# New queue order at image borders, and the gates' inner layer computed by rows of 512 pixels with stationary weights, turned through DRAM scratch

## Chip, cores and metric

One NeuronCore of a Trainium2 chip runs the whole kernel. The metric is the device time of one execution in microseconds (us). Engines: PE is TensorE, PEld its weight loads, DVE is VectorE, ACT is ScalarE, POOL is GpSimd, SP is SyncE, which issues every DMA of this kernel. TensorE's clock is granted by the chip at one of two levels, 1.2 or 2.4 GHz.

## The reference, cut to what matters

Eight images of 128 channels and 128x128 pixels pass two layers. The change touches layer 0 only; of it, the gates of the spectrum matter here:

```
x = x + _fssa(_gn(x), ...)      # layer 0, image by image
x = x + _L1_conv_ref(_gn(x))    # layer 1, a scan over the pixels
def _fssa(x, ...):
    xf = jnp.fft.fft2(x)
    ...                          # attention between channels of xf, softmax -> out_f
    g = _conv(xf.real, w1, b1)   # inner layer: 128 channels to 8, 1x1
    g = batch_norm(g); g = relu(g)
    g = sigmoid(_conv(g, w2, b2))    # 8 channels to 128
    out_f_l = abs(ifft2(g * xf))
    ...                          # q, k, v by 3x3 and 5x5 convolutions, attention, projections
```

As w1 works on channels and the transform on pixels, the kernel applies w1 to the normalised pixels first and transforms the 8 resulting channels.

## The kernel before, in words

Layer 0 handles one image after another. Each engine has one in-order program written out by hand: a function `image(b, more)`, run in a hardware loop for images 0 to 6 and once more in straight line for image 7. Engines meet at semaphores. Between images 6 and 7 there is thus no jump; after each of images 0 to 5 every engine jumps back to the top of its program.

The stages of one image, in order:

1. **Forward transform.** Per step t of 32 (four channels each), PE does `stage1(t)`: four matmuls of columns of x (`xh`, 16 channels a buffer, two buffers, loaded by SP's `columns(e, i)`) with the table `fwd` into bank t%2. ACT copies it into `AB`. `stage2(t)` makes imaginary and real part of the spectrum. DVE's `xi_copy` (L758, L759) and `xr_copy` (L764, L765) scale them into `XI`, `XR`, which lie in the SBUF tile `region`. Meanwhile the padded image `xpad` (2 MB in each of four row blocks, L1086) is normalised in place by ACT after steps 4, 12, 20 and 28.
2. **Gram.** PE multiplies the spectrum with itself, 256 matmuls of 128 columns in fp32 and some edges.
3. **Inner layer.** 128 matmuls, one a pixel column c: stationary is `xpad[:, 2:130, 2+c]` (128x128), moving is `w1t` with 8 columns. The output has rows of the image on partitions. ACT copies it to `T8`, eight matmuls with `fwd` follow, DVE copies to `A8`, `B8` (L798, L799), ten more matmuls give the 8 channels' spectrum; ACT makes the ReLU.
4. **Softmax and gates.** DVE reads the Gram (L803 to L825), with small matmuls and ACT operations between. Then five groups of gate matmuls (`gate_w`), ACT Sigmoid, DVE multiplication of XR and XI by the gates (L835).
5. **Inverse transform**, 64 matmul groups; then a loop over 32 groups of rows that mixes heads in the frequency domain and leaves `OF` in `region` (s_of).
6. **Stores and loads.** SP stores OF to DRAM as `heads` in three parts (L1111), the parts `region[kept[1]:kept[2]]` (1920 KB), `[0:kept[1]]` (1152 KB), `[kept[2]:HW]` (5120 KB). Then it loads kernels over them: WB, for the 5x5 convolutions, over the first part (L1114), WA over the second (L1116), WV and WC over the third (L1119). PE waits for WB (s_wl). ACT waits for the third store (`s_ofst[2]`) before it writes `VP[1]`, which lies there.
7. **q and k convolutions** (16 steps j), small attention, kernel merging, and the **output convolutions** (16 steps, `finish` on DVE, L1043 makes x1, L1045 its statistics). SP's `store` (L1139) writes x1.

The end of an image, in SP's order:

```
if more:
    sp.wait_ge(s_pf.sem, s_pf.at(b, NJ))
    sp.wait_ge(s_lf.sem, s_lf.at(b, NJ))
    start(b + 1)                      # four column DMAs, four xpad DMAs
sp.wait_ge(v.sem, v.at(b, LINKS))     # all of DVE's links of this image
store(NK - 1, 1)
sp.dma_start(gn2[...], col(4, 2)).then_inc(s_gst, 16)
```

DVE's next image begins with a wait for `s_gst`, since `small` and x1's buffers (in `region`) must have been read out. In the traces most matmuls carry the helper's line L1160.

Of the kernel before, what the change touches and what calls it, by code (L numbers as in the profile page):

```python
# [29 lines left out]
ACT = mybir.ActivationFunctionType  # L30
# [100 lines left out]
def layer0(nc, B, x, table, shift_d, w, wts, y_d, of_d, x1, gn2):  # L131
# [3 lines left out]
    with ctx:  # L135
# [64 lines left out]
        T8 = wk(5120, 1024).rearrange("p (w j) -> p w j", j=JG)  # L200
# [346 lines left out]
        s_t8 = count("s_hidden", 2)  # L547
        s_t8c = count("s_hidden_copied", 2)
# [111 lines left out]
        def _(dve):  # L660
# [52 lines left out]
            def image(b, more):  # L713
                n, pn, an = [0], [0], [0]

                def link(op):
                    n[0] += 1
                    op.then_inc(v.sem, 1)
                    dve.wait_ge(v.sem, v.at(b, n[0]))

                def mark(name):
                    VL[name] = n[0]
# [30 lines left out]
                dve.wait_ge(s_gst, b * 16 + 16)  # L753
# [41 lines left out]
                for hf in range(2):  # L795
                    dve.wait_ge(s_h1.sem, s_h1.at(b, hf + 1))
                    src = bk[2 + hf][:, :].rearrange("p (j u) -> p u j", j=4)
                    link(V.tensor_copy(A8[:, :, 4 * hf:4 * hf + 4], src[:, 0:HALF, :]))  # L798
                    V.tensor_copy(B8[:, 1:64, 4 * hf:4 * hf + 4], src[:, HALF:, :]).then_inc(s_h1c.sem, 1)  # L799
# [26 lines left out]
                mark("f_mix")  # L826
                for g in range(NUG):
# [243 lines left out]
        def _(sp):  # L1071
# [10 lines left out]
            def start(e):  # L1082
                for i in range(2):
                    columns(e, i)
                for i in range(4):
                    sp.dma_start(xpad[:, 2 + 32 * i:34 + 32 * i, 2:2 + P], x[bass.ds(e, 1), :, 32 * i:32 * i + 32, :].rearrange("a c h w -> (a c) h w")).then_inc(sxp[i], 16)  # L1086
# [4 lines left out]
            start(0)  # L1091
# [66 lines left out]
        def _(pe):  # L1158
# [31 lines left out]

            def image(b, more):
# [9 lines left out]

                def stage1(t):
                    pe.wait_ge(sxh[t // 4 % 2], b * 128 + 32 * (t // 8) + 32)
                    pe.wait_ge(s_ab.sem, s_ab.at(b, t - 1))
                    for c in range(4):
                        m = mm(bk[t % 2][:, c * P:(c + 1) * P], xh[:, t // 4 % 2, 4 * (t % 4) + c, :], k["fwd"], start=True, stop=True)
                    m.then_inc(s_s1.sem, 1)
# [26 lines left out]
                pe.wait_ge(s_xn.sem, s_xn.at(b, 4))  # L1234
                for hf in range(2):
                    for c in range(64 * hf, 64 * hf + 64):
                        m = mm(bk[hf][:, (c % 64) * JG:(c % 64 + 1) * JG], xpad[:, 2:2 + P, 2 + c], w1t[:, :], start=True, stop=True)
                    m.then_inc(s_t8.sem, 1)
                for hf in range(2):
                    pe.wait_ge(s_t8c.sem, s_t8c.at(b, 2))  # L1240
                    for j in range(4 * hf, 4 * hf + 4):
                        m = mm(bk[2 + hf][:, (j % 4) * P:(j % 4 + 1) * P], T8[:, :, j], k["fwd"], start=True, stop=True)
                    m.then_inc(s_h1.sem, 1)
# [7 lines left out]
                small_mm(VL["f_rows"], (bk[7][:, 0:P], k["ones"], diag[:, 0:P]))  # L1251
                pe.wait_ge(v.sem, v.at(b, VL["f_soft"]))
                mm(bk[7][:, 0:P], sq[0], k["mixc"], start=True, stop=True)
                mm(bk[7][:, P:2 * P], sq[0], k["mixs"], start=True, stop=True).then_inc(m_.sem, 1)
# [217 lines left out]
                pair_loop(pe, body)  # L1472
                small_mm(VL["gn2_mean"], (bk[7][:, 0:1], k["four"], col(0)))
# [8 lines left out]
        def _(act):  # L1482
# [9 lines left out]
            def image(b, more):  # L1492
# [19 lines left out]
                for hf in range(2):  # L1512
                    act.wait_ge(s_t8.sem, s_t8.at(b, hf + 1))
                    cp(T8[:, 64 * hf:64 * hf + 64, :], bk[hf][:, :].rearrange("p (w j) -> p w j", j=JG)).then_inc(s_t8c.sem, 1)
# [3 lines left out]
                small_act(VL["f_root"], col(10), col(8), ACT.Sqrt)  # L1518
                small_act(VL["f_max"], sq[0], sq[1], ACT.Exp, bias=col(15), accum_out=col(16))
# [793 lines left out]
def build(nc, x, out, table, shift_d, l0, l1):  # L2313
# [3 lines left out]
    def scratch(name, shape):  # L2317
# [4 lines left out]
           scratch("heads", (1, P, HW)), x1, gn2)  # L2322
# [26 lines left out]
```

## Time and profile before

| what | us |
|---|---|
| median of 3 runs (26372.1 to 30887.07) | 26372.54 |
| the profiled execution, its own time | 26375.87 |
| its span (first to last instruction) | 26373.7 |
| PE busy | 23677.5 (90%) |
| DVE busy | 19928.2 (76%) |
| ACT busy | 13080.9 (50%) |
| POOL busy | 12340.4 (47%) |

The first 12,870 us or so are layer 0, the rest is layer 1, in which nothing is changed. An engine's busy time is not its share of the path; idle times, with what ended them, tell more. An fp32 matmul appears as two records in the trace, so eight records are four fp32 matmuls.

### The profile page before, as it was taken

How to read it: one execution, taken by the hardware profiler on the slowest of the kernel's cores; microseconds unless marked ns; L12 is line 12 of the kernel's file. 1: busy time of each engine (PE TensorE's matmuls, PEld its weight loads, DVE VectorE, ACT ScalarE, POOL GpSimd, SP SyncE). 2: the span in 40 equal slices, each digit the busy share in tenths (PEclk: the TensorE clock that was granted, in tenths of full speed). 3: DMA queues.
4: the chain of work that ended last, by engine and by line, in shares of the span. 5: the costliest groups of instructions: out<-in, count | busy, mean ns of one | idle time of the engine just before them, and what ended most of it. 6: DMA issues, size and time to landing. Idle time of an engine off the chain costs nothing.

```text
span 26373.7 us, 331836 instructions
## 1 busy us (share of the span) xinstructions
PE 23677.5 (90%) x109025; PEld 14205.1 (54%) x109025; DVE 19928.2 (76%) x23929; ACT 13080.9 (50%) x18719; POOL 12340.4 (47%) x4613
## 2 busy tenths in 40 slices
PE   5998989999899998999888898988888888888888
PEld 4776877767687776867533333333333333333333
DVE  2664736556363654736899999999999999999999
ACT  1313222131321313122477777777777777777777
POOL 0000000000000000000399999999999999999998
PEclk7998989999898998989999999999999999999999
DMA  2222121222202122120344444444444444444444
GB/s 64 66 77 75 36 79 37 76 75 67 84 21 69 62 77 75 41 72 33 138 168 164 192 166 190 167 167 191 165 191 165 168 188 170 186 171 166 191 167 162
DMA packets 854279, 3179.23 MB, mean 121 GB/s; under 512 B 66089, under 2 KB 329658, under 8 KB 567354
## 3 DMA queue, kind: packets, MB, share of 16 engines
q1 hardware_dynamic: 853818, 3173.25, 32.5%
q8 instruction: 269, 4.41, 0.1%
q14 instruction: 192, 1.57, 0.0%
HBM read 2880.71 MB, written 292.30 MB: 120 GB/s over the span
## 4 chain that ended last, share of the span: by engine, by line
PE 32%; DVE 8%; issue 6%; ACT 3%; DMA 1%; DVEq 0%; ACTq 0%; POOL 0%; SPq 0%; POOLq 0%
PE yp L1961 15%; PE pj L1917 8%; DVE hid L2184 4%; DVE hid L2190 3%; PE pj L1946 2%; PE pj L1976 2%; PE pj L1934 2%; PE pj L1925 2%; PE yp L1953 1%; ACT t L2043 1%; DMA img<-x 1%; DMA bc<-bc_rows 1%; DVE delta L2226 1%; ACT xn L2057 1%; ACT du L2091 1%
## 5 line engine op out<-in xcount | busy, mean ns | idle before, releaser
L2292 POOL TENSOR_TENSOR hid<-hid,bc 128x2048 f32<-128x2048 f32 x2048 | 7815.7, 3816 | 908.2 <-DVE carry L2198 905.6
L1961 PE MATMUL yp<-hid,ident 128*128 128x512 f32 x16384 | 7346.8, 597 | 430.1 <-POOL hid L2292 430.1
L2266 POOL TENSOR_SCALAR_AFFINE_SELECT ident<-ident 128x128 f32<-128x128 f32 x1 | 0.3, 294 | 12865.4 <-DVE ident L2151 12865.4
L1961 PEld LDWEIGHTS yp<-hid,ident 128*128 128x128 f32 x16384 | 3040.8, 189 | 4629.9 <-issue 3958.9
L2184 DVE TENSOR_TENSOR_SCAN hid<-da,carry,t 128x512 f32<-128x512 f32 x3968 | 4857.7, 1266 | 111.0 <-DVE carry L2198 12.4
L2190 DVE TENSOR_TENSOR_SCAN hid<-t,carry,hid 128x512 f32<-128x512 f32 x3968 | 4828.1, 1258 | 31.7 <-ACT t L2032 30.7
L2285 POOL TENSOR_TENSOR hid<-bc,du 128x1024 f32<-128x1024 f32 x2048 | 4102.3, 2003 | 197.9 <-PE yp L1961 170.5
L1160 PE MATMUL bk<-region 128*128 128x256 f16 (+2 forms) x32688 | 3945.6, 279 | 30.6 <-ACT region L1484 19.2
L1160 PEld LDWEIGHTS bk<-region 128*128 128x128 f16 (+2 forms) x32688 | 3398.6, 119 | 610.0 <-issue 175.7
L2032 ACT ACTIVATE t<-delta,v_a 128x512 f32<-128x512 f32 x4096 | 2660.0, 681 | 1572.8 <-DVE hid L2190 1569.7
L1917 PE MATMUL pj<-xn,w_x 128*128 128x512 f32 x4096 | 2375.6, 734 | 1078.4 <-ACT xn L2057 1030.5
L1160 PE MATMUL bk<-work,region 128*128 128x256 f16 x27336 | 3146.3, 273 | 24.2 <-DVE region L1023 20.5
L1160 PEld LDWEIGHTS bk<-work,region 128*128 128x128 f16 x27336 | 2641.5, 99 | 493.2 <-issue 72.5
L2043 ACT ACTIVATE t<-bc 128x1024 f32<-128x1024 f32 x2048 | 2096.5, 1024 | 1438.8 <-DVE hid L2184 1387.1
L2020 ACT ACTIVATE da<-delta,v_a 128x512 f32<-128x512 f32 x4096 | 2703.4, 707 | 0.3 <-DVE delta L2226 0.3
L2170 DVE TENSOR_TENSOR t<-t,du 128x1024 f32<-128x1024 f32 x2048 | 2478.9, 1210 | 258.4 <-ACT t L2043 258.4
L1484 ACT ACTIVATE work<-bk 128x512 f32<-128x512 f32 (+1 forms) x1720 | 944.5, 588 | 2792.4 <-PE bk L1160 2590.4
L1484 ACT ACTIVATE work<-work 128x512 f32<-128x512 f32 (+3 forms) x656 | 696.5, 1062 | 3288.8 <-DVE work L924 1414.9
L1917 PEld LDWEIGHTS pj<-xn,w_x 128*128 128x128 f32 x4096 | 942.5, 237 | 2458.4 <-issue 2448.5
L905 DVE COPY work<-bk 128x512 f32<-128x512 f32 x640 | 442.7, 692 | 1885.0 <-PE bk L1160 1884.4
L1484 ACT ACTIVATE region<-work 128x512 f32 (+2 forms) x384 | 646.7, 1684 | 2068.8 <-DVE work L894 1572.1
L1160 PE MATMUL bk<-work 128*128 128x128 f32 (+1 forms) x7168 | 1193.6, 325 | 39.7 <-DMA work<-in_shift_d 21.2
(286 smaller groups left out, 23596.1 us busy)
## 6 DMA issues: line engine op xcount, KB each, us to landing
bc<-bc_rows SPq DMA_DIRECT2D x1024, 2048.0 KB, 7.2
work<-in_shift_d SPq DMA_DIRECT2D x256, 512.0 KB, 3.8
work<-in_x SPq DMA_DIRECT2D x256, 256.0 KB, 2.7
work<-in_x SPq DMA_DIRECT2D x128, 512.0 KB, 4.8
xpad<-in_x SPq DMA_DIRECT2D x32, 2048.0 KB, 18.6
gated<-work SPq DMA_DIRECT2D x256, 256.0 KB, 2.2
region<-gated SPq DMA_DIRECT2D x256, 256.0 KB, 3.0
region<-heads SPq DMA_DIRECT2D x256, 256.0 KB, 3.2
```

What stands on the lines that cost most here:

```text
L1160: mm = lambda *args, **kw: nc.tensor.matmul(*args, skip_group_check=True, **kw)
L1484: cp = lambda o, i, f=ACT.Copy, **kw: nc.scalar.activation(o, i, f, **kw)
L1917: m = nc.tensor.matmul(pj[h][:, :], w_x[:, t, h * P:(h + 1) * P], xn[:, t:t + CH], start=(t == 0), stop=(t == K4 - 1))
L1961: m = nc.tensor.matmul(yp[:, h, :], ident[:, :], hid[:, k % 4, n, :], start=False, stop=(g == G - 1 and n == 3), skip_group_check=True)
L2020: m = nc.scalar.activation(da[:, k % 2, j, :], delta[:, q, h, :], ACT.Exp, scale=v_a[:, h, 4 * g + j:4 * g + j + 1])
L2032: m = nc.scalar.activation(t1[:, j, :], delta[:, q, h, :], ACT.Exp, scale=v_a[:, h, 4 * g + 2 + j:4 * g + 3 + j])
L2043: nc.scalar.activation(t0[:, :, :], bc[:, g, 0, 0:2, :], ACT.Copy).then_inc(s_t0.sem, 1)
L2170: nc.vector.tensor_tensor(t0[:, :, :], t0[:, :, :], du[:, q, h, :].unsqueeze(1).broadcast_to([P, 2, CH]), ALU.mult).then_inc(s_m.sem, 1)
L2184: m = nc.vector.tensor_tensor_scan(hid[:, k % 4, j, :], da[:, k % 2, j, :], t0[:, j, :], first(j), ALU.mult, ALU.add)
L2190: m = nc.vector.tensor_tensor_scan(o, t1[:, j - 2, :], o, first(j), ALU.mult, ALU.add)
L2285: nc.gpsimd.tensor_tensor(hid[:, k % 4, 2:4, :], bc[:, g, 0, 2:4, :], du[:, q, h, :].unsqueeze(1).broadcast_to([P, 2, CH]), ALU.mult).then ...
L2292: nc.gpsimd.tensor_tensor(hid[:, k % 4, :, :], hid[:, k % 4, :, :], bc[:, g, 1, :, :], ALU.mult).then_inc(s_hc.sem, 1)
```

## The change

Queue order. SP's `start` is split. At the end of an image only the four column DMAs go out early; after the last x1 store and the gn2 store comes the first block of xpad, and the other three blocks follow inside the next image, one behind each of the column loads i = 2, 3, 4. DVE's first copy waits for the x1 stores and not for gn2's; the gn2 wait comes before the softmax. PE does `stage1` of steps 0 and 1 of the next image before the last two small matmuls of this one. The three heads stores are issued one by one, each with the load that overwrites it right behind.

Inner layer. The stationary operand is now w1t (128x8), the moving one 512 pixels, four matmuls to one PSUM bank at partitions 0, 32, 64, 96. ACT copies each bank to `hidden` (two halves), SP stores it with four DMAs of 8 partitions x 2 KB to DRAM scratch `hidden_d`, and one DMA reads it back with image rows on partitions. A bank's half of `hidden` is used again when its stores have landed; the wait is PE's. The softmax chain of DVE, PE and ACT now lies ahead of the `A8`, `B8` copies.

```diff
@@ vector
-                dve.wait_ge(s_gst, b * 16 + 16)
+                for i in range(2):
+                    dve.wait_ge(s_x1st[i], b * (8 * NK) + 16)
                 for t in range(NK):
                     xi_copy(t)
                     xr_copy(t)
...
+                dve.wait_ge(s_gst, b * 16 + 16)
...
-                for hf in range(2):
-                    dve.wait_ge(s_h1.sem, s_h1.at(b, hf + 1))
...
                 mark("f_mix")
+                for hf in range(2):
+                    dve.wait_ge(s_h1.sem, s_h1.at(b, hf + 1))
@@ sync
+            first_columns(0)
+            padded_rows(0, 0)
             def image(b, more):
                 for i in range(2, 8):
                     sp.wait_ge(s_s1.sem, s_s1.at(b, 4 * (i - 1)))
                     columns(b, i)
+                    if i < 5:
+                        padded_rows(b, i - 1)
+                sp.wait_ge(s_st.sem, s_st.at(b, NK))
+                for q in range(8):
+                    sp.wait_ge(s_t8c.sem, s_t8c.at(b, q + 1))
+                    for i in range(4):
+                        c0 = 2048 * q + 512 * i
+                        sp.dma_start(hidden_d[:, c0:c0 + 512], hidden[32 * i:32 * i + JG, q % 2, :]).then_inc(s_t8st[q % 2], 16)
+                for i in range(2):
+                    sp.wait_ge(s_t8st[i], b * 256 + 256)
+                sp.dma_start(T8, hidden_d[:, :].rearrange("j (h w) -> h j w", w=P)).then_inc(s_t8l, 16)
...
-                for i, (c0, c1) in enumerate(((kept[1], kept[2]), (0, kept[1]), (kept[2], HW))):
+                def heads_part(i, c0, c1):
                     sp.dma_start(of_d[0:1, :, c0:c1].rearrange("a c n -> (a c) n"), region[:, c0:c1]).then_inc(s_ofst[i], 16)
+                heads_part(0, kept[1], kept[2])
                 sp.wait_ge(s_ofst[0], b * 16 + 16)
                 sp.dma_start(WB, wts[:, kept[1]:kept[2]]).then_inc(s_wl, 16)
+                heads_part(1, 0, kept[1])
                 sp.wait_ge(s_ofst[1], b * 16 + 16)
                 sp.dma_start(WA, wts[:, kept[0]:kept[1]]).then_inc(s_wla, 16)
+                heads_part(2, kept[2], HW)
                 sp.wait_ge(s_ofst[2], b * 16 + 16)
...
-                    start(b + 1)
+                    first_columns(b + 1)
                 sp.wait_ge(v.sem, v.at(b, LINKS))
                 store(NK - 1, 1)
                 sp.dma_start(gn2[bass.ds(b, 1), :, :].rearrange("a c n -> (a c) n"), col(4, 2)).then_inc(s_gst, 16)
+                if more:
+                    padded_rows(b + 1, 0)
@@ tensor
-                stage1(0)
                 for t in range(NK):
-                    if t + 1 < NK:
-                        stage1(t + 1)
+                    if 0 < t < NK - 1:
+                        stage1(b, t + 1)
                     stage2(t)
...
                 pe.wait_ge(s_xn.sem, s_xn.at(b, 4))
+                for q in range(8):
+                    pe.wait_ge(s_t8c.sem, s_t8c.at(b, q - 1))
+                    if q >= 2:
+                        pe.wait_ge(s_t8st[q % 2], b * 256 + 64 * (q // 2))
+                    for i in range(4):
+                        r = 2 + 16 * q + 4 * i
+                        m = mm(bk[q % 2][32 * i:32 * i + JG, :], w1t[:, :], xpad[:, r:r + 4, 2:2 + P], start=True, stop=True)
+                    m.then_inc(s_t8.sem, 1)
+                small_mm(VL["f_rows"], (bk[7][:, 0:P], k["ones"], diag[:, 0:P]))
+                pe.wait_ge(v.sem, v.at(b, VL["f_soft"]))
+                mm(bk[7][:, 0:P], sq[0], k["mixc"], start=True, stop=True)
+                mm(bk[7][:, P:2 * P], sq[0], k["mixs"], start=True, stop=True).then_inc(m_.sem, 1)
+                pe.wait_ge(s_t8l, b * 16 + 16)
-                    for c in range(64 * hf, 64 * hf + 64):
-                        m = mm(bk[hf][:, (c % 64) * JG:(c % 64 + 1) * JG], xpad[:, 2:2 + P, 2 + c], w1t[:, :], start=True, stop=True)
...
                 pair_loop(pe, body)
+                if more:
+                    pe.wait_ge(s_fd.sem, s_fd.at(b, NK - 1))
+                    stage1(b + 1, 0)
+                    stage1(b + 1, 1)
                 small_mm(VL["gn2_mean"], (bk[7][:, 0:1], k["four"], col(0)))
@@ scalar
-                for hf in range(2):
-                    act.wait_ge(s_t8.sem, s_t8.at(b, hf + 1))
-                    cp(T8[:, 64 * hf:64 * hf + 64, :], bk[hf][:, :].rearrange("p (w j) -> p w j", j=JG)).then_inc(s_t8c.sem, 1)
+                for q in range(8):
+                    act.wait_ge(s_t8.sem, s_t8.at(b, q + 1))
+                    cp(hidden[:, q % 2, :], bk[q % 2][:, :]).then_inc(s_t8c.sem, 1)
+                    if q == 4:
+                        small_act(VL["f_root"], col(10), col(8), ACT.Sqrt)
+                small_act(VL["f_max"], sq[0], sq[1], ACT.Exp, bias=col(15), accum_out=col(16))
```

## Rows read from the trace of the kernel before

**Rows 1.** Waits, 0 to 12870 us: who waited for whom, total us, times, longest.

```profile
PE bk L1160 <- DMA region<-kernels: 222.1, 7, 31.8
DVE region L758 <- DMA gn<-small: 210.5, 7, 31.5
```

**Rows 2.** Timeline, border of images 1 and 2: start, us, engine, line, operation [idle <-releaser].

```profile
3399.36 5.59 SPq L1080 DMA_DIRECT2D work<-in_x  x4
...
3402.69 1.88 PE L1160 MATMUL bk<-region,work 128*128 128x512 f32 x4
...
3405.05 23.97 SPq L1086 DMA_DIRECT2D xpad<-in_x  x4
...
3413.63 0.15 DVE L749 TENSOR_SCALAR small<-small 128x1 f32<-128x1 f32 x1
...
3419.14 3.56 PE L1160 MATMUL bk<-ctab,work 128*128 128x128 f32 x16 [6.36 <-issue]
...
3429.28 6.82 SPq L1139 DMA_DIRECT2D x<-region  x1
...
3444.26 0.16 DVE L758 TENSOR_TENSOR region<-bk,norm_rows 128x4 f32<-128x4 f32 x1 [30.47 <-DMA gn<-small]
...
3445.20 3.78 PE L1160 MATMUL bk<-work,ctab 128*128 128x260 f32 x8 [17.27 <-DVE region L765]
```

**Rows 3.** Timeline of PE, border of images 6 and 7 (no jump).

```profile
11287.29 3.76 PE L1160 MATMUL bk<-ctab,work 128*128 128x128 f32 x16
...
11319.61 3.75 PE L1160 MATMUL bk<-work,ctab 128*128 128x260 f32 x8 [22.06 <-DVE region L765]
```

**Rows 4.** Timeline, image 0, PE's wait for its third column block.

```profile
309.25 1.01 PE L1160 MATMUL bk<-ctab,work 128*128 128x128 f32 x3 [12.68 <-DMA work<-in_x]
```

**Rows 5.** Windows: stretch, length, PE, PEld, DVE, ACT, POOL busy, clock, DMA share, GB/s.

```profile
3598.00:3658.50 60.50, 59.90 (x259) 59.80 (x257) 0.00 (x0) 1.17 (x2) 0.00 (x0) 0.52 0.00 1
...
3405.00:3437.00 32.00, 9.97 (x52) 9.19 (x52) 6.77 (x18) 2.59 (x5) 0.00 (x0) 0.72 1.00 293
4029.00:4044.00 15.00, 0.00 (x0) 0.00 (x0) 9.92 (x9) 2.84 (x1) 0.00 (x0) 0.50 1.01 415
```

**Rows 6.** Timeline of PE and ACT, image 2, inner layer to first gates.

```profile
3598.09 59.81 PE L1160 MATMUL bk<-w1t,xpad 128*128 128x8 f32 x256
3658.58 4.19 PE L1160 MATMUL bk<-ctab,work 128*128 128x128 f32 x16 [0.69 <-ACT work L1484]
...
3667.71 0.57 PE L1160 MATMUL bk<-ctab,B 128*104 128x128 f32 x2
...
3674.84 4.70 PE L1160 MATMUL bk<-gate_w,relu_r 105*128 105x512 f32 x8
...
3679.64 1.28 ACT L1484 ACT_TABLE_LOAD   x1 [6.39 <-PE bk L1160]
```

**Rows 7.** Timeline, image 2, heads stored and kernels loaded.

```profile
4028.49 0.33 SPq L1114 DMA_DIRECT2D region<-kernels  x1
...
4032.09 3.46 DVE L900 SCALAR_TENSOR_TENSOR work<-work 128x3168 f16<-128x3168 f32 x1 [2.98 <-ACT work L1484]
...
4044.44 2.84 ACT L1484 ACTIVATE region<-work 128x3168 f16<-128x3168 f32 x1 [12.45 <-DMA heads<-region]
...
4049.67 0.69 PE L1160 MATMUL bk<-B,relu_r 128*128 128x64 f32 x2 [31.75 <-DMA region<-kernels]
...
4072.68 0.68 PE L1160 MATMUL bk<-region 128*64 128x64 f32 x8
```

**Rows 8.** The page's DMA issues: count, KB each, median us to landing.

```profile
work<-in_x SPq DMA_DIRECT2D x128, 512.0 KB, 4.8
xpad<-in_x SPq DMA_DIRECT2D x32, 2048.0 KB, 18.6
...
x<-region SPq DMA_DIRECT2D x256, 256.0 KB, 2.0
...
bc_rows<-rows SPq DMA_DIRECT2D x256, 64.0 KB, 1.6
```

More of the change, by code:

```diff
@@ L128, in at, with layer0 @@
         return b * self.per + self.per + n
-def layer0(nc, B, x, table, shift_d, w, wts, y_d, of_d, x1, gn2):
+def layer0(nc, B, x, table, shift_d, w, wts, y_d, of_d, hidden_d, x1, gn2):
     _, at = constants()
@@ L199, in layer0 @@
         AB = wk(4096, 1024).rearrange("p (s c u) -> p s c u", s=2, u=P)
-        T8 = wk(5120, 1024).rearrange("p (w j) -> p w j", j=JG)
+        T8 = wk(5120, 1024).rearrange("p (j w) -> p j w", j=JG)
+        hidden = wk(6400, 1024).rearrange("p (q n) -> p q n", q=2)
         gates = wk(0, UG * P).rearrange("p (u c) -> p u c", c=P)
@@ L546, in layer0 @@
         s_gram = count("s_gram", 1)
-        s_t8 = count("s_hidden", 2)
-        s_t8c = count("s_hidden_copied", 2)
+        s_t8 = count("s_hidden", 8)
+        s_t8c = count("s_hidden_copied", 8)
+        s_t8st = [sem(f"s_hidden_stored_{i}") for i in range(2)]
+        s_t8l = sem("s_hidden_columns_loaded")
         s_h1 = count("s_hidden_stage1", 2)
@@ L792, in roots @@
                     link(V.reciprocal(col(12, w_), col(10, w_)))
-                for hf in range(2):
-                    dve.wait_ge(s_h1.sem, s_h1.at(b, hf + 1))
-                    src = bk[2 + hf][:, :].rearrange("p (j u) -> p u j", j=4)
-                    link(V.tensor_copy(A8[:, :, 4 * hf:4 * hf + 4], src[:, 0:HALF, :]))
-                    V.tensor_copy(B8[:, 1:64, 4 * hf:4 * hf + 4], src[:, HALF:, :]).then_inc(s_h1c.sem, 1)
                 dve.wait_ge(s_gram.sem, s_gram.at(b, 1))
@@ L826, in image @@
                 mark("f_mix")
+                for hf in range(2):
+                    dve.wait_ge(s_h1.sem, s_h1.at(b, hf + 1))
+                    src = bk[2 + hf][:, :].rearrange("p (j u) -> p u j", j=4)
+                    link(V.tensor_copy(A8[:, :, 4 * hf:4 * hf + 4], src[:, 0:HALF, :]))
+                    V.tensor_copy(B8[:, 1:64, 4 * hf:4 * hf + 4], src[:, HALF:, :]).then_inc(s_h1c.sem, 1)
                 for g in range(NUG):
@@ L1080, in columns, with first_columns, padded_rows @@
                     sp.dma_start(xh[:, i % 2, 8 * hf:8 * hf + 8, :], x[bass.ds(e, 1), c0:c0 + 8, :, :].rearrange("a c h w -> h (a c) w")).then_inc(sxh[i % 2], 16)
-            def start(e):
+            def first_columns(e):
                 for i in range(2):
                     columns(e, i)
-                for i in range(4):
+            def padded_rows(e, i):
                     sp.dma_start(xpad[:, 2 + 32 * i:34 + 32 * i, 2:2 + P], x[bass.ds(e, 1), :, 32 * i:32 * i + 32, :].rearrange("a c h w -> (a c) h w")).then_inc(sxp[i], 16)
@@ L1090, in _ @@
             sp.wait_ge(s_edge, 4)
-            start(0)
+            first_columns(0)
+            padded_rows(0, 0)
             def image(b, more):
@@ L1189, in _, with stage1 @@
                 step(0)
+            def stage1(b, t):
+                pe.wait_ge(sxh[t // 4 % 2], b * 128 + 32 * (t // 8) + 32)
+                pe.wait_ge(s_ab.sem, s_ab.at(b, t - 1))
+                for c in range(4):
+                    m = mm(bk[t % 2][:, c * P:(c + 1) * P], xh[:, t // 4 % 2, 4 * (t % 4) + c, :], k["fwd"], start=True, stop=True)
+                m.then_inc(s_s1.sem, 1)
+            stage1(0, 0)
+            stage1(0, 1)
             def image(b, more):
@@ L1200, in small_mm @@
                     x_.then_inc(m_.sem, 1)
[L1202 to L1207, printed above, removed]
                 def stage2(t):
@@ L1234, in image @@
                 pe.wait_ge(s_xn.sem, s_xn.at(b, 4))
-                for hf in range(2):
-                    for c in range(64 * hf, 64 * hf + 64):
-                        m = mm(bk[hf][:, (c % 64) * JG:(c % 64 + 1) * JG], xpad[:, 2:2 + P, 2 + c], w1t[:, :], start=True, stop=True)
-                    m.then_inc(s_t8.sem, 1)
-                for hf in range(2):
-                    pe.wait_ge(s_t8c.sem, s_t8c.at(b, 2))
+                for q in range(8):
[11 more added lines that the diff above has]
+                pe.wait_ge(s_t8l, b * 16 + 16)
+                for hf in range(2):
                     for j in range(4 * hf, 4 * hf + 4):
-                        m = mm(bk[2 + hf][:, (j % 4) * P:(j % 4 + 1) * P], T8[:, :, j], k["fwd"], start=True, stop=True)
+                        m = mm(bk[2 + hf][:, (j % 4) * P:(j % 4 + 1) * P], T8[:, j, :], k["fwd"], start=True, stop=True)
                     m.then_inc(s_h1.sem, 1)
@@ L1249, in image @@
                     mm(o, B8[:, u0:u0 + UG, :].rearrange("p u j -> p (u j)"), k["cs"][:, P:], start=False, stop=True).then_inc(s_h2.sem, 1)
[L1251 to L1254, printed above, removed]
                 gate_flat = gate_w[:, :, :].rearrange("p u c -> p (u c)")
@@ L1511, in image @@
                         normalise(t // 8)
-                for hf in range(2):
-                    act.wait_ge(s_t8.sem, s_t8.at(b, hf + 1))
-                    cp(T8[:, 64 * hf:64 * hf + 64, :], bk[hf][:, :].rearrange("p (w j) -> p w j", j=JG)).then_inc(s_t8c.sem, 1)
+                for q in range(8):
[4 more added lines that the diff above has]
+                small_act(VL["f_max"], sq[0], sq[1], ACT.Exp, bias=col(15), accum_out=col(16))
                 for g in range(NUG):
@@ L1517, in image @@
                     cp(relu_r[0:UG * JG, g, :], bk[g // 4][0:UG * JG, (g % 4) * P:(g % 4 + 1) * P], ACT.Relu, bias=gate_sb[:, 1:2], scale=gate_sb[:, 0:1]).then_inc(s_rel.sem, 1)
-                small_act(VL["f_root"], col(10), col(8), ACT.Sqrt)
-                small_act(VL["f_max"], sq[0], sq[1], ACT.Exp, bias=col(15), accum_out=col(16))
                 for g in range(NUG):
@@ L2321, in build @@
     layer0(nc, B, x, table, shift_d, l0, scratch("kernels", (P, (T3W + 3 * T5W) * P)), scratch("gated", (1, P, P, P)),
-           scratch("heads", (1, P, HW)), x1, gn2)
+           scratch("heads", (1, P, HW)), scratch("hidden", (JG, HW)), x1, gn2)
     layer1(nc, x1, gn2, *(l1[n] for n in _L1), scratch("bc_rows", (2, 32, 512)), out.rearrange("b c i j -> b c (i j)"), B)
```

## The prediction

> **What bounds the kernel now.** The page gives PE as busiest, but a busy share says nothing of where an edit pays, so I read first who waited for whom in layer 0, and then the timeline around the longest waits of PE. Two waits recur once an image. PE waits for the kernels WB some 31.8 us (seven such waits here; the eighth is put down to "issue"), and DVE waits for the store of `gn2` up to 31.5 us at each of the seven borders [rows 1]. The reader is to see in the border's timeline [rows 2] that this second wait is a queue's: DVE has its last value at 3413.8, but SP is still issuing the four xpad DMAs (3405.05 to 3429), then x1's store takes 6.82 us to be issued behind them, and DVE goes on only at 3444.26. PE ran two steps ahead meanwhile and then stood 17.27 us. The third place is a stretch without waits: the inner layer takes 60.5 us, PE and its weight loads 99% busy, the granted clock 0.52 of full, DVE idle [rows 5, 6]. Its cost is 256 loads of 128x128 fp32 weights for 8 columns each. All three are on PE's path, so each us saved there is a us of the image, unless a next wait is close. Layer 1 is untouched.
>
> **Border, six times with a jump.** After the change x1's store goes out at 3413.9 with only 2 MB of columns ahead of it, issued from 3399.36 and, at 293 GB/s, landed by 3408 [rows 2, 5]. It lands in 2.0 us [rows 8], by 3416. Next late is then the jump itself: PE shows 6.36 us of "issue" before its first matmul of the new image at 3419.14 [rows 2], which I take to be the return to the top of the loop. I charge ACT the same, as no row shows its jump; bounds are 0 (the wait was something of the old queue) and 6.4. ACT then copies AB(0) by 3420.2 and PE starts stage2(0), cold: 3.8 us as the row at 3445.20. Stage1 of step 2, still half slow, 1.5; stage2(1) 1.9; stage1(3) 0.9 to 1.05 (halves of the slow 3.78 and 3.56). Stage2 of step 2 starts at 3428.4 where it started at 3445.20: 16.8 us saved, 101 for six. PE's early stage1 (8 fp32 matmuls, 3.6 us slow) fits before the small matmul that waits for DVE's statistics until 3410.8, since columns 0 landed by about 3405. Cost nothing; without that cover it would delay the last link by 3 us.
>
> **Border 6 to 7, straight.** There stage1 followed the last small matmul at once [rows 3]. AB(0) is copied at about 11288.5, stage2(0) ends by 11292.4, step 2 starts near 11296.9, not 11319.61: 22.7 us.
>
> **Image 0.** PE waited 12.68 us for its third column block, behind 8 MB of xpad [rows 4]. Only 2 MB stand before it now: 12.7 us saved. In all later images the blocks are interleaved: per four steps 1 MB of columns and 2 MB of xpad, 3.15 MB, 10.7 us at 293 GB/s [rows 5]; a step is 1.9 + 0.9 us warm, so four last 11.2. It just fits; zero cost, bound 0 to 3 us an image. ACT normalises block 0 after step 4, at about 3432; issued at 3415, it should be there by 3427, by the 7 us that its bytes take and as much again for queueing.
>
> **Inner layer.** New are 32 matmuls of 512 fp32 columns. Such records last 1.88 us for four, so 0.47 each and 0.94 a matmul [rows 2]; M = 3.76 us a bank, in the open. PE starts bank q only when the stores of q-2 have landed: 3.76 + ACT's copy 0.6 + semaphores 0.2 + the fourth issue + its landing. An issue costs 0.33 at least [rows 7] and 1.4 for a 512 KB column block (5.59 / 4, rows 2); I take 0.5, near the small end, so 1.5 until the fourth. Landing: 64 KB to DRAM take 1.6, 256 KB 2.0 [rows 8]; I take 1.7 for 16 KB. The sum is 7.8 us per two banks, over the 7.5 of PE alone, so the stores pace it. Bank 6 starts at 23.4, bank 7 ends at 30.9; its copy, issues and landing add 4.0, the load back of 512 KB in 512-byte rows 4.8, as the columns [rows 8]. T8 is there at 39.7 where it was after 60.5: 20.8 saved, 166 in eight images. Bounds for landing and issue (1.6 with 0.33, 2.5 with 1.0) give 22 to 12 us. The T8 matmuls behind it stay at half clock as they were (4.19), because PE idles before them.
> The Trainium skill, "DMA: Bandwidth & Descriptors", section Rules for kernel authors, speaks against such stores: transfers under 64 KB pay mostly overhead. Its fixed cost of about 2.0 us a DMA (an estimate from that page) would lengthen three round trips and the last landing by 0.3 each, 10 us in all over the run. No run yet shows 16 KB stores.
>
> **Softmax chain.** It stood between the h2 matmuls (end 3668.3) and the gates (3674.84) [rows 6]. Now DVE, PE and ACT do it during the bank loop and the load back, some 9 us of cover for the 4.2 us after the last bank. Gates begin 6.5 us earlier, but 8 records at half clock last 7.5, not 4.7; I take 5.5 (bounds 3.7 to 6.5): 44 us. DVE's A8 copies find DVE free, and SP's stores queue before nothing that is due.
>
> **Heads and kernels.** WB was queued at 4028.49 behind 6.3 MB of stores and landed about 4049.6. Alone it is 1.97 MB at 415 GB/s, 4.7 us [rows 5], plus 1.7: 4035. DVE finishes the first points at 4035.55 [rows 7]; that is next late, and PE starts at 4035.8 and not 4049.67: 13.9. The third store is later, however: WB and store 1 end at 4037.7, WA and store 2 (6.42 MB) 17.1 us later, 4054.8, ten after the old 4044.4. ACT waits for that, then 2.84 us of points, a square and a copy, until 4058.9; PE's first small Gram, 23.0 us after its start, comes at 4058.8. So the cover is just used up; I take 13.5 (bounds 9 to 14): 108 us.
>
> **Sum.** 101 + 23 + 13 + 166 + 44 + 108 = 455 us. The profiled execution took 26375.87, with a span of 26373.7; its median sibling 26372.54, the difference is nothing. 26372.5 - 455 = 25,917 us.
>
> **Rivals.**
> *The four matmuls of a bank overlap.* Each uses 8 columns of weights and its own quarter of PSUM partitions. If the second of a matmul's records may run beside the first of the next, M is 5 records, 2.35 us: 6.4 per pair, T8 at 32.5, 58 us more saved: 25,859. If all run together, M is 0.94, 4.9 per pair and T8 at 25.5: 25,803. For it: different output quarters. Against: no row of this trace has two such neighbours. Chance 0.25, shared evenly.
> The Trainium skill, "TensorEngine Tiling (Array Packing)", section Key Properties, states that different tiles can execute in parallel; no run so far shows it for fp32.
> *Half clock.* The present stage drew 0.52 [rows 5] although PE was called busy. If 8 columns of weights don't hold the clock either, M is 7.5, T8 is at 69, 8.5 later than now: 234 us lost from the sum, 26,151. Against: it streams 512 columns. Chance 0.08.
> *Columns starve behind xpad.* The fit above is 10.7 in 11.2. If image 0's wait of 12.68 moves into each image: 26,018. Against: two blocks of slack at the start. Chance 0.1.
> *Slower than before.* The store round trip takes the place of the weight loads. It decides from the point where a pair of banks lasts 27 us (a landing of 21 us and not 1.7), as the inner stage would then last 97 us and eat the 57 us an image. Landings of 18.6 exist [rows 8], but behind 6 MB of other traffic; the DMA share in this stage is 0.00 [rows 5]. At a landing of 25 us: 26,660. Chance 0.02.
> *It does not do what it says at the borders*, say an engine's own jump keeps everyone as long: 100 us less, 26,017. Chance 0.05.
> The forecast itself has 0.5.
>
> **Range and chances.** From the full overlap, 25,803, to the bounds of the sum with one of the stalls, 26,080: about 8 in 10. A measurement of this kernel tells 2%, 527 us, from no change. Faster by more than that (under 25,845) needs the overlap or every bound at its good end: 0.24. Within 2%: 0.73. Slower by over 2%: 0.03.
>
> **What would show it.** Border: the first L758 copy about 7 us after PE's last small matmul plus 4 cold, near 10 us after DVE's last link instead of 30.5, and no wait for gn. Inner layer: first bank to T8 matmuls 40 us, records of 0.47, clock near 1.0 in the loop, a gap of about 9 us before T8. Gates: no small matmuls between h2 and gate_w. Heads: PE's wait for WB 18 us, ACT's for the third store longer than 12.45. Image period 1578 less about 55. I am wrong if the loop's period differs from 3.9 us a bank, if the jump hides a longer fetch, or if the third store holds the Gram.

## The result, and the profile after

The changed kernel takes 25783.61 us (median of 4 runs, 25772.88 to 25788.08) against 26372.32 on the same chip: a ratio of 0.9777, 95% interval 0.9758 to 0.9796, 589 us less. (One of the four runs of the kernel before took 30887.07 us, was disturbed and does not enter the ratio.) The profiled execution took 25786.19 us, with a span of 25784.3. The forecast, 25,917, was 133 us too high, and the time lies 19 us under the low end of the range. All of it is in layer 0: POOL, which waits for the end of layer 0 before its first instruction of layer 1, waits 12275.0 us where it waited 12865.4.

Waits of the changed kernel in layer 0, then its timeline at the border of images 1 and 2, which answers to [rows 1] and [rows 2]:

```profile
ACT region L1518 <- DMA heads<-region: 166.8, 6, 28.2
PE bk L1184 <- issue: 155.3, 9, 19.2
...
PE bk L1184 <- DMA hidden<-work: 50.8, 42, 2.5
...
DVE region L760 <- DMA x<-region: 4.6, 1, 4.6
```

```profile
3264.02 2.05 PE L1184 MATMUL bk<-ctab,work 128*128 128x128 f32 x16 [2.48 <-DMA work<-in_x]
...
3266.68 1.02 DVE L738 BATCH_NORM_AGGREGATE small<-stats 128x2 f32<-128x192 f32 x1
...
3270.31 0.15 DVE L752 TENSOR_SCALAR small<-small 128x1 f32<-128x1 f32 x1
3270.49 0.37 SPq L1161 DMA_DIRECT2D x<-region  x1
3271.05 0.37 SPq L1170 DMA_DIRECT2D gn<-small  x1
3271.52 0.93 SPq L1093 DMA_DIRECT2D xpad<-in_x  x1
3272.54 1.08 ACT L1518 ACTIVATE work<-bk 128x512 f32<-128x512 f32 x2 [2.65 <-issue]
...
3273.37 3.77 PE L1184 MATMUL bk<-work,ctab 128*128 128x260 f32 x8 [3.92 <-ACT work L1518]
...
3277.18 0.16 DVE L760 TENSOR_TENSOR region<-bk,norm_rows 128x4 f32<-128x4 f32 x1 [6.72 <-PE bk L1184]
...
3281.60 1.89 PE L1184 MATMUL bk<-work,ctab 128*128 128x260 f32 x8
```

DVE's wait for the store of `gn` is gone from the waits. The reader is to see SP's rows: x1's store is issued 0.18 us after DVE's last link begins and takes 0.37, where it took 6.82 in the old queue [rows 2]. DVE copies again 6.72 us after the link, not 30.47. What is left is ACT's 2.65 of "issue" (the jump) and a first stage2 that is still slow (3.77). From DVE's last aggregate of one image to the first bank of the next, the stretch lasts 22.8 us less here, and 22.5 on the mean of the six borders with a jump.

The inner layer, the gates behind it, and the heads, in the timeline of image 2, and then windows; they answer to [rows 5 to 7]:

```profile
3432.32 1.91 PE L1184 MATMUL bk<-xpad,w1t 128*8 128x512 f32 x16
...
3434.06 18.16 SPq L1112 DMA_DIRECT2D hidden<-work  x32
...
3436.59 3.45 PE L1184 MATMUL bk<-xpad,w1t 128*8 128x512 f32 x16 [2.36 <-DMA hidden<-work]
...
3441.64 1.05 PE L1184 MATMUL bk<-xpad,w1t 128*8 128x512 f32 x8 [1.61 <-DMA hidden<-work]
...
3445.86 1.89 PE L1184 MATMUL bk<-xpad,w1t 128*8 128x512 f32 x8 [0.66 <-DMA hidden<-work]
...
3453.43 0.39 SPq L1115 DMA_DIRECT2D work<-hidden  x1
...
3457.89 3.79 PE L1184 MATMUL bk<-ctab,work 128*128 128x128 f32 x16 [2.90 <-DMA work<-hidden]
...
3467.03 3.05 PE L1184 MATMUL bk<-gate_w,relu_r 105*128 105x512 f32 x8
...
3473.25 5.98 DVE L841 TENSOR_TENSOR region<-region,work 128x1664 f32<-128x1664 f32 x2 [10.66 <-ACT work L1518]
...
3825.64 0.66 PE L1184 MATMUL bk<-B,relu_r 128*128 128x64 f32 x2 [18.87 <-issue]
...
3828.68 0.43 SPq L1130 DMA_DIRECT2D heads<-region  x1
...
3848.52 2.84 ACT L1518 ACTIVATE region<-work 128x3168 f16<-128x3168 f32 x1 [27.70 <-DMA heads<-region]
...
3852.51 0.93 PE L1184 MATMUL bk<-region 128*64 128x64 f32 x8 [4.24 <-ACT region L1518]
...
3861.41 5.71 PE L1184 MATMUL bk<-region 128*128 128x256 f16 x53
```

```profile
3432.32:3457.89 25.57, 13.61 (x72) 2.51 (x71) 7.64 (x27) 6.65 (x12) 0.00 (x0) 0.71 0.18 41
3457.89:3473.25 15.36, 11.21 (x44) 9.19 (x44) 1.70 (x4) 4.88 (x10) 0.00 (x0) 0.70 0.00 1
```

The first row holds two banks, 16 records, in 1.91 us: 0.95 a bank. Eight records of 0.47 us one after the other would be 3.76, so the four matmuls of a bank ran at once. Two more readings of the trace say the same: the bank's first four records begin within 0.02 us (3432.32 to 3432.34), the other four 0.44 later, and ACT copies the bank at 3433.43, 1.11 us after its first record. Later banks last 1.05 or up to 1.89; the granted clock of the stretch is 0.71 on the mean. PE no longer sets the pace: it waits for a landing at 42 of the 48 banks that must. SP's 32 stores stretch over 18.16 us; the four of a bank are issued 0.34 us apart, and between banks SP waits for ACT's copy. The T8 matmuls come 25.57 us after the first bank (24.6 on the mean of the eight images), where the old layer had them after 60.5 [rows 6]. At the heads PE's wait for WB carries the name "issue" (18.87 us here; 31.75 before, under WB's load). PE starts 12.9 us sooner relative to the first store, but ACT waits 27.70 us for the third store where it waited 12.45 [rows 7], and PE stands 4.24 us at its small Gram, which had no wait before. The matmuls behind that wait are slower at first, too. The next part of PE's program, in the row at 3861.41, stands in the trace of the kernel before as:

```profile
4080.00 5.71 PE L1160 MATMUL bk<-region 128*128 128x256 f16 x53
```

The first store was issued at 3811.31 here and 4022.46 there, which makes 50.1 us against 57.5. Of the 12.9 us 7.4 are left.

### The profile page after: what moved, and what is told of

It is laid out like the page before. It is cut to its first block, busy times and chain, and to the rows that moved or that the text cites. A ratio compares the mean times of both kernels' runs of the same rounds, so it can differ in the third digit from the quotient of the medians.

```text
span 25784.3 us, 329198 instructions
## 1 busy us (share of the span) xinstructions
PE 23262.4 (90%) x107489; PEld 13716.6 (53%) x107489; DVE 19930.4 (77%) x23929; ACT 13106.8 (51%) x18767; POOL 12340.0 (48%) x4613
## 4 chain that ended last, share of the span: by engine, by line
PE 32%; DVE 8%; issue 6%; ACT 3%; DMA 1%; DVEq 0%; ACTq 0%; POOL 0%; SPq 0%; POOLq 0%
PE yp L1996 16%; PE pj L1952 8%; DVE hid L2219 4%; DVE hid L2225 3%; PE pj L1981 2%; PE pj L2011 2%; PE pj L1969 2%; PE pj L1960 2%; PE yp L1988 1%; ACT t L2078 1%; DMA img<-x 1%; DVE delta L2261 1%; DMA bc<-bc_rows 1%; ACT xn L2092 1%; ACT du L2126 1%
## 5 line engine op out<-in xcount | busy, mean ns | idle before, releaser
L2301 POOL TENSOR_SCALAR_AFFINE_SELECT ident<-ident 128x128 f32<-128x128 f32 x1 | 0.3, 295 | 12275.0 <-DVE ident L2186 12275.0
L1518 ACT ACTIVATE work<-bk 128x512 f32<-128x512 f32 (+2 forms) x1768 | 972.3, 589 | 2240.2 <-PE bk L1184 2021.9
```

The costliest lines, as they stand in the source:

```text
L1518: cp = lambda o, i, f=ACT.Copy, **kw: nc.scalar.activation(o, i, f, **kw)
```

## The experiments

All were timed beside the kernel before. One chip served the first four; a second those with the softmax chain behind, the old xpad order, the old `gn` wait and the split store; a third those without the early stage1, with two queues and with both. The kernel before took 26370, 26365 and 26373 us on them. The changed kernel itself was timed on another occasion, beside a kernel before of 26372, so differences from it are uncertain by up to 8 us. On the second chip the run with the old `gn` wait (25784.08) shows no such offset.

My theory after seeing the result (theory A where an expectation names it) is that the four matmuls of a bank run at once and that this made the inner layer short; its rival is that this overlap decides nothing, since the stores pace the loop anyway. For the other parts the rival is the forecast's own term.

**Without the overlap.** `w1z` holds the eight columns between 96 zeros on each side, so each matmul writes 104 PSUM rows and adds its own eight. Count, columns streamed and stores stay.

```
-  m = mm(bk[q % 2][32 * i:32 * i + JG, :], w1t[:, :], xpad[...], start=True, stop=True)
+  m = mm(bk[q % 2][0:96 + JG, :], w1z[:, 96 - 32 * i:192 + JG - 32 * i], xpad[...], start=(i == 0), stop=(i == 3))
```

> The changed kernel, but the inner layer's four matmuls of a bank have 104 columns of weights, all zero but for the eight of w1 in another strip each, and accumulate over the whole bank; they can't run beside each other. Result unchanged. Theory A, the missed step is that the four matmuls of 8 columns overlap (0.95 us a bank in the changed kernel's trace): M becomes 3.76 us, the T8 matmuls begin 39.7 us after the Gram and not 25.6, +113 us, 25,897 us. Rival B, the loop is paced by the stores of the banks alone and the matmuls hide in any case: within 15 us of 25,784.

Measured: 25863.78 us (25854.49 to 25869.99), ratio 0.9807 [0.9791, 0.9823], 80 us slower than the changed kernel. Its timeline in image 2, and the stage's window:

```profile
3454.05 27.76 PE L1187 MATMUL bk<-xpad,w1z 128*104 128x512 f32 x64
...
3458.33 25.43 SPq L1115 DMA_DIRECT2D hidden<-work  x32
...
3484.98 0.39 SPq L1118 DMA_DIRECT2D work<-hidden  x1
...
3488.80 3.78 PE L1187 MATMUL bk<-ctab,work 128*128 128x128 f32 x16 [2.69 <-DMA work<-hidden]
```

```profile
3454.05:3492.00 37.95, 31.90 (x87) 14.33 (x86) 8.49 (x29) 6.64 (x12) 0.00 (x0) 0.92 0.12 28
```

The same 64 records now run one behind the other: 0.43 us each, 3.45 a bank, and T8 is there after 34.75 us, 9.2 later than with the overlap. Over the eight images of both traces the difference is 83 us, next to the 80 measured. That shows the overlap and its price; the expectation's rival, that the stores pace the loop in any case, is refuted. The run changes two things together, the width of the weights and the rows that are written, so it does not say which of them ends the overlap. It also shows a second error of the forecast: even without overlap T8 comes at 34.75 and not at 39.7. PE never stood idle between banks (the round trip fits behind two banks, 6.9 us), the fetch back took 3.8 us and not 4.8, and a bank 3.45 and not 3.76.

**Each part undone.** Three kernels take one part back to its old form: the inner layer together with the softmax chain's place; the border (SP's xpad order, the early stage1, DVE's wait for `gn`); the order of the heads' stores and kernels' loads.

```
-  for q in range(8): for i in range(4): mm(bk[q % 2][32 * i:32 * i + JG, :], w1t, xpad rows)   # 32 x 512 columns
+  for hf in range(2): for c in range(64 * hf, 64 * hf + 64): mm(bk[hf][8 columns], xpad[:, 2:2 + P, 2 + c], w1t)
```

> The changed kernel with inner layer and softmax order as before: 128 matmuls of 8 columns, no DRAM turn; the queue order stays new. By the rows of both traces this gives back 34.8 us of the inner layer and 8.8 of the way to the gates per image, 349 us: 26,133 us. If the two halves of the change share their gain (the borders having profited from the shorter inner layer), less than 300.

> The changed kernel with the old order at the borders (all four xpad blocks before the last x1 store, DVE waiting for the gn2 store before its first copy, PE without the early steps 0 and 1). Theory A: back come 22.8 us at each of six borders, about 27 at the seventh and 12.7 in image 0: +177 us, 25,961 us. By the forecast's terms it would be 137 us: 25,921.

> The changed kernel with the three heads stores issued together again. By the traces this term is worth 7.4 us an image, since PE's earlier start (12.9) is partly given back at the first small Gram: +59 us, 25,843 us. By the forecast's term (13.5 an image): +108, 25,892.

Measured: inner layer and chain old 26147.93 (26142.3 to 26152.61), ratio 0.9915 [0.9899, 0.9932], so the part is worth 364 us; border old 25952.09 (25946.93 to 25954.49), 0.9842 [0.9826, 0.9858], 168 us; heads old 25846.08 (25837.44 to 25849.48), 0.9801 [0.9785, 0.9817], 62 us. Together 595, next to the 589 of the whole: the parts hardly touch each other. Each lies near its sum from the timelines (357, 172 and 59, worked out below), and not at the forecast's terms of 210, 137 and 108 us.

**Softmax chain behind the ReLU again**, with the new inner layer.

```
-  small_mm(VL["f_rows"], ...); ... mm(bk[7][:, P:2 * P], sq[0], k["mixs"], ...)   # ahead of the wait for T8
+  the same lines behind the h2 matmuls; DVE's and ACT's steps of the chain likewise
```

> The changed kernel with the softmax chain back behind the ReLU; the new inner layer stays. From the last T8 matmul to DVE's first gate multiply the changed kernel takes 15.36 us and the one before 24.14. If those 8.8 us are the chain's, this kernel is 8.8 x 8 = 70 us slower than the changed one, 25,854. The forecast's term was 5.5 an image: 25,828. Rival: the chain only filled a wait elsewhere in the new order (its small matmuls and ACT functions also cost a few us in the bank loop), and the time is within 15 us of 25,784.

Measured: 25849.18 (25846.78 to 25853.72), ratio 0.9804 [0.9788, 0.982], 65 us slower. In image 2:

```profile
3472.20 3.78 PE L1184 MATMUL bk<-ctab,work 128*128 128x128 f32 x16 [7.14 <-DMA work<-hidden]
...
3483.44 0.49 PE L1184 MATMUL bk<-work,ctab 128*128 128x128 f32 x2 [1.89 <-DVE work L817]
...
3487.03 1.22 PE L1184 MATMUL bk<-ctab,work 128*128 128x128 f32 x4 [3.10 <-DVE work L823]
...
3488.04 4.96 PE L1184 MATMUL bk<-gate_w,relu_r 105*128 105x512 f32 x8
...
3496.18 5.97 DVE L841 TENSOR_TENSOR region<-region,work 128x1664 f32<-128x1664 f32 x2 [5.84 <-ACT work L1518]
```

From T8 to DVE's first gate multiply are 23.98 us, 15.36 in the changed kernel. Over the eight images this stretch is 66 us longer, which is the whole difference: the chain is worth 8 us an image. Its small matmuls bring two waits of PE with them, 1.89 and 3.10.

**The border's three edits apart.** One kernel has SP's old xpad order alone, one DVE's old wait for `gn`, one PE without the early stage1.

```
-  padded_rows(0, 0); in the loop: if i < 5: padded_rows(b, i - 1); at the border: padded_rows(b + 1, 0) behind the stores
+  for i in range(4): padded_rows(b + 1, i)     # right behind first_columns(b + 1)
```

> The changed kernel, but SP issues all four xpad blocks together as before: in front of image 0's loop, and at a border behind the first column blocks. Early stage1 and DVE's moved wait stay. If SP's queue is what held the border, DVE's statistic store again waits behind 8 MB of xpad, but now DVE's first copies do not wait for it, only for the first x1 store: both stores are issued late. Expected: DVE's wait returns, here for the x1 store, some 15 us at each of 7 borders, plus image 0's 12.7: 120 us slower, 25,900. If moving the wait for gn behind the copies and the early stage1 is what pays, the queue order is worth only image 0's 12.7: 25,797.

```
+  dve.wait_ge(s_gst, b * 16 + 16)     # ahead of xi_copy(0)
```

> The changed kernel, but DVE waits for the statistic store of gn ahead of its first copy, as before; SP's new order stays. The store is issued 0.56 us behind x1's first and in a short queue, so if the queue was the cause the wait costs nothing: 25,784 within 10. If the moved wait is what pays, DVE waits some 2 us longer at each of 7 borders, 14 us or more: 25,800 and above.

```
-  stage1(b + 1, 0); stage1(b + 1, 1)   # behind the last Z of image b, ahead of the jump
+  stage1(b, 0) at the top of the image, stage1(b, t + 1) in the loop
```

> The changed kernel without the early stage1: PE starts the new image's stage1(0) only behind the jump, and stage1(t+1) in the loop as before; SP's new order and DVE's moved wait stay. In the changed kernel ACT copies the first bank 2.65 us behind the jump and PE's first stage2 starts at 3273.37. Without the early part PE jumps, then does two half slow stage1 (about 3.6 us) and ACT copies behind them: 3 to 4 us later at each of 7 borders, plus at most 2 us in image 0: 25,784 + 25 = 25,809. The forecast had PE's own jump at 6.36 us with the early part in place; if PE's jump is 6.4 where ACT's is 2.65, this kernel is slower by 6.5 x 7 = 46: 25,830. If neither matters, 25,784 within 8.

Measured: xpad order old 25945.88 (25938.19 to 25950.67), ratio 0.984 [0.9824, 0.9856], 162 us slower, which is nearly the whole border; `gn` wait old 25784.08 (25777.15 to 25787.6), 0.9779 [0.9762, 0.9795], nothing; no early stage1 25800.35 (25797.82 to 25802.81), 0.9782 [0.9766, 0.9799], 17 us slower, between the expectation's 25 for a short jump of PE and its "nothing", and far from the 46 of a jump of 6.4. In the traces the seven borders are longer by 8 us together; the rest of the 17 lies in other stages, within what repeats of a kernel differ by. The old xpad order, in the waits and the timeline of its border of images 1 and 2:

```profile
ACT work L1517 <- issue: 32.6, 6, 7.0
...
DVE region L760 <- DMA x<-region: 203.8, 7, 29.8
```

```profile
3301.24 23.52 SPq L1093 DMA_DIRECT2D xpad<-in_x  x4
...
3309.51 0.15 DVE L752 TENSOR_SCALAR small<-small 128x1 f32<-128x1 f32 x1
...
3315.92 1.08 ACT L1517 ACTIVATE work<-bk 128x512 f32<-128x512 f32 x2 [6.83 <-issue]
...
3325.02 7.13 SPq L1160 DMA_DIRECT2D x<-region  x1
...
3338.84 0.16 DVE L760 TENSOR_TENSOR region<-bk,norm_rows 128x4 f32<-128x4 f32 x1 [29.18 <-DMA x<-region]
```

The wait has only changed its name: DVE no longer waits for `gn`, but 29.18 us for x1's store, behind the same four xpad DMAs. So it is the queue that held the border, and moving the wait alone would have done nothing. The expectation counted some 15 us a border and was too low; 162 less image 0's 12.7 are 21 for each of seven, and DVE's wait is 22.5 us longer (29.18 against 6.72). The jump grew as well, but it is not on this path: ACT is through with it at 3315.92, 23 us before DVE's copy. It takes ACT 6.83 us here, 32.6 in six (4.2 to 7.0), and 2.65 in the changed kernel, 16.4 in six. The windows around the two jumps, the old xpad order first:

```profile
3301.00:3333.00 32.00, 11.02 (x52) 9.54 (x52) 7.06 (x18) 2.48 (x5) 0.00 (x0) 0.73 1.01 295
```

```profile
3256.00:3272.00 16.00, 8.47 (x58) 6.25 (x56) 7.16 (x18) 0.20 (x1) 0.00 (x0) 0.91 0.64 195
```

The DMA share is 1.01 there and 0.64 in the changed kernel. PE's jump agrees, in the kernel without the early stage1, where the queue is short: 3.64 us of "issue" (3.1 to 3.7 in six) and not the 6.36 of [rows 2] (5.3 to 6.6 in six).

```profile
3278.12 3.77 PE L1184 MATMUL bk<-ctab,work 128*128 128x128 f32 x16 [3.64 <-issue]
```

**The third heads store split.** The 1280 KB over which VP[1] is written go out first, right behind WB's load, and ACT waits for them alone.

```
+  heads_part(3, kept[4], HW)           # behind WB's load, ahead of store 1 and WA
-  heads_part(2, kept[2], HW)
+  heads_part(2, kept[2], kept[4])
-  act.wait_ge(s_ofst[2], b * 16 + 16)
+  act.wait_ge(s_ofst[3], b * 16 + 16)
```

> The changed kernel with its third heads store cut in two: the 1280 KB that VP[1] is written over is stored right behind the load of WB, ahead of store 1 and WA, and ACT waits for that part alone; the rest goes out last. If the heads' saving is only 7.4 us an image because the third store lands 23 us after its issue and ACT waits 27.70 us for it, that wait goes: 1280 KB at some 300 to 400 GB/s land 4 to 5 us behind WB, well before ACT asks for it, and PE's 4.24 us at the small Gram go too. Expected 5.5 us an image, 44 in eight: 25,740. The rival: WB's landing or WA's (now later by 1280 KB, 3 to 4 us) holds PE instead, and the time stays at 25,784 or rises.

Measured: 25750.65 (25740.6 to 25755.71), ratio 0.9766 [0.975, 0.9782], 33 us faster than the changed kernel. Its timeline in image 2, first store at 3811.28 (3811.31 in the changed kernel):

```profile
3825.72 0.66 PE L1186 MATMUL bk<-B,relu_r 128*128 128x64 f32 x2 [18.98 <-issue]
...
3830.76 2.84 ACT L1520 ACTIVATE region<-work 128x3168 f16<-128x3168 f32 x1 [9.98 <-DVE work L900]
...
3849.61 0.68 PE L1186 MATMUL bk<-region 128*64 128x64 f32 x8
```

ACT starts its points at 3830.76 and not 3848.52, and now waits for DVE, not for a store. PE's small Gram has no wait and comes 2.9 us sooner; the weights of the next such matmuls are loaded 4.5 us sooner (3861.96 against 3866.44). 4.5 x 8 = 36 of the expected 44. So the third store had cost the heads what the forecast had counted as gain.

**Stores from two queues.** ACT issues half of each bank's four stores.

```
+  act.wait_ge(s_t8c.sem, s_t8c.at(b, q + 1))
+  for i in range(2, 4):
+      act.dma_start(hidden_d[:, c0:c0 + 512], hidden[32 * i:32 * i + JG, q % 2, :]).then_inc(s_t8st[q % 2], 16)
```

> The changed kernel, but of the four 16 KB stores of each bank ACT issues two in its own queue, behind its copy, and SP the other two. In the changed kernel SP takes 18.16 us for the 32 issues, 0.57 each and 2.3 a bank, and PE waits for a landing at nearly every bank, 50.8 us in eight images. If SP's issue pace is what sets the loop now, two issues side by side take 1.1 us from each of the eight banks, less ACT's own time for issuing: T8 is there 4 to 8 us sooner, 30 to 60 us in the run, 25,725 to 25,755. Rival: the landing alone sets the pace (two banks need copy 0.6, issue, some 2 us of landing, semaphores), or ACT's waits for its own copy take the gain back: 25,784 within 10, or slower.

> The split third heads store (33 us faster by itself than the changed kernel) together with the stores of the inner layer from two queues. The two stand in stages of an image that do not touch, so the savings should add: 25,751 less what the two queues bring by themselves, 25,700 to 25,720 if that is 30 to 50 us.

Measured: 25768.92 (25758.53 to 25777.49), ratio 0.9771 [0.9755, 0.9787]: 15 us less than the changed kernel, the size of the spread between runs. The expected 30 to 60 us did not come. With the split store as well 25724.06 (25719.26 to 25729.62), ratio 0.9755 [0.9738, 0.9771], 59.6 us less than the changed kernel and the fastest version here; that is 12 us more than the 33 and 15 of the two edits, while repeats of the two-queue kernel differ by 19, and just above the 25,700 to 25,720 expected. The two-queue kernel in image 2:

```profile
3430.74 1.91 PE L1184 MATMUL bk<-xpad,w1t 128*8 128x512 f32 x16
...
3432.48 13.80 SPq L1112 DMA_DIRECT2D hidden<-work  x16
...
3434.61 1.05 PE L1184 MATMUL bk<-xpad,w1t 128*8 128x512 f32 x8 [1.96 <-DMA hidden<-work]
...
3451.83 3.77 PE L1184 MATMUL bk<-ctab,work 128*128 128x128 f32 x16 [1.77 <-DMA work<-hidden]
```

Here T8 comes after 21.1 us, 4.5 sooner. But images differ. From the first store's issue to the load's, the eight images take 16.8 to 19.4 us in the changed kernel (mean 18.3) and 15.3 to 17.5 with two queues (mean 16.4): 1.9 x 8 = 15 us. PE still waits for landings (42 such waits in both kernels, 50.8 us in the changed one and 42.8 with two queues). The expectation had read SP's 0.57 us a store as the price of an issue, where most of it was SP's own wait for copies. Two issues less in a row save 0.7 us a bank (they begin 0.34 us apart), and part of that is lost again: from the last issue of a bank to the bank that PE starts on its landing 1.5 to 1.6 us pass in the changed kernel and 1.8 to 1.9 with two queues. Why is not shown.

## Why the prediction was wrong

**The step that failed** is the inner layer's term, "M = 3.76 us a bank, in the open". A bank took 0.95 to 1.9, since the four matmuls run at once, as the full-overlap rival said with its 0.94 a bank and T8 at 25.5 (25.57 measured in image 2, 34.9 us saved and not 20.8). T8 comes 35.9 us sooner on the mean of all eight images, 287 us instead of 166. The undone overlap gives some 80 of the 121 us between them. The rest, some 40, is in sizes that the forecast took a little long: a bank one behind the other 3.45 and not 3.76, the fourth issue 1.03 us after the first and not 1.5, a landing 1.5 to 1.6 and not 1.7, the fetch back 3.8 in the run without the overlap (4.5 in the changed kernel) and not 4.8. The rival was priced right for this stage. That its total of 25,803 lies only 19 us from the measured time is luck: it stood on the forecast's other terms, whose errors of +36, +26 and -49 nearly cancel. Wrong as well was the sign "clock near 1.0 in the loop": it was granted 0.71, and 0.92 in the run without the overlap, in which PE has no pauses.

**Border with the jump**, 16.8 forecast, 22.8 measured: mechanism right, size off. PE's 6.36 of "issue" had been taken for the jump's fixed price and charged to ACT. It was 2.65 once SP's queue and the DMA engines were not full. That is 3.7 of the 6.0 missed. The other 2.3 were left out of the sum: it ends where stage2 of step 2 starts, but before the change that stage2 and the stage1 behind it, after 17.27 us of waiting, lasted 3.78 and 1.47 us, and in the changed kernel, with PE running already, 1.89 and 1.05 (the row at 3281.60). Six borders make 36 us. The straight border and image 0 came as forecast (21.5 and 13.8 against 22.7 and 12.7), and the columns did not starve.

**Softmax chain**, 5.5 forecast, 8.8 measured in image 2 and 8 by the experiment. From T8 to the first gate matmul 9.1 us are left of 16.3, so 7.1 and not 6.5 saved. The forecast then took 1 us back, because eight gate records at half clock would last 7.5; they took 3.05, at a granted clock of 0.70 on the mean of the stage, and DVE's multiply came another 1.6 us sooner. The chain now runs while PE waits for stores and for the load back anyway.

**Heads**, 13.5 forecast, 7.4 measured: the one term that was too large. PE's start was 12.9 us sooner against 13.9. The forecast saw that the third store would land later, at 4054.8, and called the cover "just used up". Counted from the first store's issue (4022.46 before, 3811.31 after) that is 32.3 us; ACT could start on its landing after 37.2 (store 1 had landed 1.8 us later than forecast, the third took some 3 more), and the 4.9 us were in the open: ACT's points set the Gram. The split store shows it.

**The sum.** By the timelines 13.8 + 6 x 22.8 + 21.5 + 287 + 70 + 59 = 588 us, next to 590 in layer 0 and 589 in the time. The errors against the forecast: +121 inner layer, +36 border, +26 chain, -49 heads, nothing net elsewhere: 134 us. These sums take image 2 for all at the border and the heads; over all eight images of the two traces the stretches give 170 for the borders, 287, 71, 8 between the gates and the heads, and 54 for the heads, 590 as well. Two of the forecast's smaller sums were off by themselves. With a landing of 21 us a pair of banks does last 27, but the last landing grows too, and T8 comes at 117 us and not 97; "slower than before" starts at a landing near 16. And the chance of 0.24 for "faster by more than 2%" counted both overlap cases, though the half overlap's 25,859 lies above 25,845. Left open: how the granted clock falls in the bank loop differs from image to image (banks of 1.05 and of 1.89 us), and no run here fixes it.

## What to carry to other kernels

When matmuls with few weight columns write different quarters of the PSUM rows, price both "one behind the other" and "at once", and let a case in which the matmul becomes free tell you which wait is next (here the store's round trip). A wait for a small DMA is a question about its queue: look at what SP issued before it, and move that; moving the wait behind other work only renames it. And when a load is moved ahead of a store, follow the last store of the group to whoever overwrites its source: splitting that store was worth half as much as the reordering itself (33 and 62 us).

## What the runs showed of the hardware

- Four fp32 matmuls of 128 rows by 8 columns into four quarters of the PSUM rows ran in 0.95 us a bank, eight records of 512 columns, against 3.45 a bank when 104 columns of weights wrote overlapping rows (which of the two ends the overlap is not shown). The Trainium skill, "TensorEngine Tiling (Array Packing)", section Key Properties, says that different tiles can execute in parallel; these runs agree, for fp32 as well.
- An engine's jump to the top of its loop lasted 6.83 us on ACT (4.2 to 7.0 at six borders) while the four xpad DMAs were queued, the DMA share at 1.01, and 2.65 (2.65 to 2.9) at a share of 0.64; on PE 5.3 to 6.6 and 3.1 to 3.7. Why is not shown.
- SP issued the four 16 KB stores of a bank 0.34 us apart, and PE's next bank began 1.5 to 1.6 us after the last issue (1.8 to 1.9 when ACT's queue took half of them). The Trainium skill, "DMA: Bandwidth & Descriptors", section Rules for kernel authors, which the forecast weighed, says that transfers under 64 KB pay mostly overhead. The trace agrees, as PE's waits for these landings came to 50.8 us, and the stage still saved 287. The landing of 2.0 us that the forecast drew from that page as an estimate is longer than what was measured.
- SP took 0.37 us to issue x1's last 256 KB store when only the four column DMAs had gone out before it, and 6.82 (7.13 in the run with the old xpad order) behind four xpad DMAs of 2 MB.
